# A fused cross-attention and segmented self-attention layer on one core: the cross weighted sum with its two operands exchanged, and GpSimd's rotary sums ahead of its clamps

## What is computed

```python
q, k, v = query @ Wq + bq, key_in @ Wk + bk, key_in @ Wv + bv        # split in 16 heads of 8
scores = einsum('bhqd,bhkd->bhqk', q, k) / sqrt(8)
scores = 0.5 * scores * mask + 0.5 * scores
attn = softmax(clip(scores, -50, 50), axis=-1)
context = einsum('bhqk,bhkd->bhqd', attn, v)                         # 128 queries, 77 keys
x = layernorm(query + context @ Wo + bo) * gamma + beta
```

## Time and profile before

| | us |
|---|---|
| median of 3 runs | 1788.41 |
| lowest and highest | 1788.29, 1788.67 |
| the profiled execution's own time | 1788.83 |
| its span in the trace | 1787.0 |
| TensorE matmul busy | 1626.6 (91%) |
| VectorE busy | 1205.8 (67%) |
| GpSimd busy | 837.2 (47%) |
| ScalarE busy | 779.9 (44%) |

### The profile page before, as it was taken

One profiled execution on the slowest core, in us unless ns is written; L12 is line 12 of the kernel. 1 busy time (PEld: TensorE's weight loads), 2 busy tenths in 40 slices (PEclk: granted clock), 3 DMA queues, 4 the chain that ended last, 5 costly groups with the idle time before them and its releaser, 6 DMA issues.

```text
span 1787.0 us, 61340 instructions
## 1 busy us (share of the span) xinstructions
PE 1626.6 (91%) x23267; PEld 1398.3 (78%) x23267; DVE 1205.8 (67%) x3087; ACT 779.9 (44%) x1869; POOL 837.2 (47%) x1170
## 2 busy tenths in 40 slices
PE   4899999999999999999999999999999999999997
PEld 3687787887887877878888787877877878878776
DVE  4566766766766766766766767667667667667664
ACT  2444444444444444444444344344444444444443
POOL 3345445445445445345345445454454454454452
PEclk9999999999999999999999999999999999999999
DMA  6000000000000000000000000000000000000000
GB/s 163 13 15 11 8 13 11 8 13 11 8 13 11 8 11 9 11 11 8 13 11 8 13 11 8 13 11 8 13 11 8 13 11 8 13 11 8 13 6 6
DMA packets 32411, 25.54 MB, mean 14 GB/s; under 512 B 8117, under 2 KB 31178, under 8 KB 32266
## 3 DMA queue, kind: packets, MB, share of 16 engines
q1 hardware_dynamic: 32394, 25.30, 5.4%
HBM read 20.82 MB, written 4.46 MB: 14 GB/s over the span
## 4 chain that ended last, share of the span: by engine, by line
PE 33%; issue 33%; DVE 18%; POOL 14%; POOLq 1%; DMA 1%; DVEq 0%; SPq 0%; ACT 0%; ACTq 0%
PE psum L852 9%; PE psum L816 6%; PE psum L818 6%; POOL ra L406 5%; DVE ra L631 4%; PE psum L826 4%; DVE rb L634 4%; POOL kmask L417 2%; DVE z L640 2%; POOL st L468 2%; DVE mx L701 2%; POOL z L413 2%; POOL st L421 2%; PE psum L962 2%; PE psum L835 1%
## 5 line engine op out<-in xcount | busy, mean ns | idle before, releaser
L406 POOL TENSOR_TENSOR ra<-ra,rb 128x512 f32<-128x512 f32 x256 | 322.1, 1279 | 0.1
L701 DVE TENSOR_REDUCE mx<-psum 128x4 f32<-128x324 f32 x256 | 108.7, 487 | 198.4 <-PE psum L841 198.4
L640 DVE TENSOR_TENSOR z<-psum,wT 77x512 f32<-77x512 f32 x256 | 163.6, 678 | 99.6 <-PE psum L808 99.6
L631 DVE TENSOR_TENSOR ra<-psum,rope 128x512 f32<-128x512 f32 x256 | 175.0, 683 | 81.9 <-PE psum L800 77.5
L413 POOL TENSOR_SCALAR z<-z 77x512 f32<-77x512 f32 x256 | 152.8, 611 | 149.4 <-DVE z L640 149.4
L468 POOL TENSOR_TENSOR st<-st,nhalf 128x1 f32<-128x1 f32 x64 | 37.5, 586 | 363.3 <-DVE st L726 363.3
L523 ACT ACTIVATE z<-z 77x512 f32<-77x512 f32 x256 | 152.0, 638 | 125.3 <-POOL z L413 125.3
L852 PE MATMUL psum<-qT,kall 64*81 64x64 f32 x4096 | 176.0, 236 | 23.6 <-DVE mx L701 23.6
L826 PE MATMUL psum<-cross_w,ra 128*128 128x128 f32 x1024 | 147.7, 277 | 48.4 <-POOL ra L406 47.8
L852 PEld LDWEIGHTS psum<-qT,kall 64*81 64x81 f32 x4096 | 158.4, 148 | 36.3 <-DVE mx L701 32.0
L816 PE MATMUL psum<-z,v 77*32 77x128 f32 x2048 | 179.7, 278 | 0.7 <-DVE z L640 0.7
(11 more groups left out here) (129 smaller groups left out, 3419.1 us busy)
## 6 DMA issues: line engine op xcount, KB each, us to landing
seq_in<-in SPq DMA_DIRECT2D x64, 166.5 KB
out<-out_sb SPq DMA_DIRECT2D x64, 64.0 KB, 1.6
maskT<-in SPq DMA_DIRECT2D x64, 38.5 KB
vall<-memv_dram SPq DMA_DIRECT2D x128, 4.0 KB, 1.9
ctx_all<-in SPq DMA_DIRECT2D x5, 320.0 KB, 12.1
wqkv<-in SPq DMA_DIRECT2D x1, 1536.0 KB, 9.5
ctx_all<-in SPq DMA_DIRECT2D x3, 288.0 KB, 10.8
stage<-in SPq DMA_DIRECT2D x1, 648.0 KB
```

The costliest lines, as they stand in the source:

```text
L406: nc.gpsimd.tensor_tensor(ra[:, sl], ra[:, sl], rb[:, sl], ALU.add).then_inc(rot_ready, 1)
L631: V.tensor_tensor(ra[:, sl].rearrange("n (h d) -> n h d", h=8), p, rope[:, 0, :].unsqueeze(1).broadcast_to([S, 8, DH]), ALU.mult)
L640: V.tensor_tensor(z0[:, 4 * t:4 * t + 4, :], cross_at(f"score{t}")[0:S2, :].rearrange("k (h q) -> k h q", h=4), wT[:].unsqueeze(1).broadca ...
```

## The change

- `v0` becomes 77 x 16 heads x 9 columns: eight value columns and one of ones, set to 1.0 once; `ones0` is gone, and the set-up zeroes one tile less.
- `weigh_cross` takes 64 queries of a head's exponentials as the stationary operand (77 x 64) and the head's nine columns as the moving one, into partitions 0 to 63 or 64 to 127 of bank `pv`. That is again 32 fp32 matmuls (64 records). Each group waits for its own exponentials.
- The result has queries on partitions. `context` takes a 128 x 16 reciprocal and multiplies into a new tile `c0` (128 x 128); it now stands on VectorE ahead of the maxima's reductions.
- TensorE transposes `c0` between `maxima(1)` and `scores(0)`, and ScalarE copies the transpose into `c0T` between `values(1)` and the copy of the shift. `c0T @ Wo` stays where it was. The list of bank tasks gains `c0T`.
- GpSimd adds all four rotary pairs in a row, then does the four clamps.

```diff
@@ -34,7 +34,7 @@
 NSEG = S // SEG
 NPM, NM = 16, 16
 PRE = 1 + NPM
-VROW = HD0 * GROUP + HD0
+VROW = HD0 + 1
 KEYS = SEG + PRE
 VW = DH + 1
 DFF = 341
@@ -157,10 +157,10 @@
         k0T = sb("k0T", [D, S2])
 
         kmask = sb("kmask", [D, GROUP, S2])
-        v0 = sb("v0", [S2, GROUP, GROUP * VROW])
-        ones0 = sb("ones0", [S2, GROUP * VROW])
+        v0 = sb("v0", [S2, H, VROW])
         z0 = sb("z0", [S2, H, S])
-        rden0 = sb("rden0", [128, S])
+        rden0 = sb("rden0", [S, H])
+        c0 = sb("c0", [S, D])
         c0T = sb("c0T", [D, S])
         r0 = sb("r0", [S, D])
         t0g = sb("t0g", [S, D])
@@ -281,7 +282,7 @@
 
         cross_at, cross_fill, cross_filled, cross_free = banks(ctx, nc, psum, "cross", 0, 2, [
             ("qkv", qkv0_ready, 1, 1), *[(f"score{t}", z_ready, t + 1, 4) for t in range(4)],
-            ("pv", c0T_ready, 1, 1), ("wo", r_ready, 1, 1)])
+            ("pv", c0_ready, 1, 1), ("c0T", c0T_ready, 1, 1), ("wo", r_ready, 1, 1)])
         self_at, self_fill, self_filled, self_free = banks(ctx, nc, psum, "self", 2, 4, [
             ("xnT", xnT_lo_ready, 1, 1), ("q0", rope_ready, 1, 4), ("k0", rope_ready, 2, 4), ("v0", v_ready, 1, 2),
             ("q1", rope_ready, 3, 4), ("k1", rope_ready, 4, 4),
@@ -387,13 +388,13 @@
         @block.gpsimd
         def _(pool):
             nc.gpsimd.memset(nhalf[:], -0.5).then_inc(nhalf_set, 1)
-            for t in (v0, ones0, *vall, half_gate, tanh_gate):
+            for t in (*vall, half_gate, tanh_gate):
                 nc.gpsimd.memset(t[:], 0.0).then_inc(zeros_step, 1)
-            pool.wait_ge(zeros_step, 6)
-            nc.gpsimd.memset(ones0[:].rearrange("k (r w) -> k r w", r=GROUP)[:, :, 0:HD0], 1.0).then_inc(zeros_set, 1)
+            nc.gpsimd.memset(v0[:], 1.0).then_inc(zeros_set, 1)
+            pool.wait_ge(zeros_step, 4)
             for s in range(NSEG):
                 nc.gpsimd.memset(vall[s][:, 0:H * VW].rearrange("n (h w) -> n h w", h=H)[:, :, DH:VW], 1.0).then_inc(zeros_step, 1)
-            pool.wait_ge(zeros_step, 8)
+            pool.wait_ge(zeros_step, 6)
             for s in range(NSEG):
                 mem_col = vall[s][SEG:SEG + 1, 0:H * VW].rearrange("n (h w) -> n h w", h=H)[:, :, DH:VW]
                 nc.gpsimd.memset(mem_col, float(NM)).then_inc(zeros_set, 1)
@@ -423,17 +424,11 @@
                     if first(a):
                         pool.wait_ge(setup_dve, 4)
                         nc.gpsimd.tensor_tensor(pool_st[:, 1:2], pool_st[:, 0:1], nhalf[0:B, :], ALU.pow).then_inc(setup_pool, 1)
-                    rotated("q0")
-                    rotated("k0")
-                if c is not None:
-                    clamped(0)
-                    clamped(1)
-                if a is not None:
-                    rotated("q1")
-                    rotated("k1")
-                if c is not None:
-                    clamped(2)
-                    clamped(3)
+                    for name in QK:
+                        rotated(name)
+                if c is not None:
+                    for t in range(4):
+                        clamped(t)
                 if a is not None:
                     if first(a):
                         pool.wait_ge(setup_act, 3)
@@ -534,8 +529,7 @@
                     wait(act, (kmask_ready, c))
                     nc.scalar.activation(k0T[:], p[:, S:S + S2], ACT.Identity, bias=cols[:, BK:BK + 1]).then_inc(k0_ready, 1)
                     nc.scalar.activation(q0T[:], p[:, 0:S], ACT.Identity, bias=cols[:, BQ:BQ + 1])
-                    copy(v0[:].rearrange("k g (r w) -> k g r w", r=GROUP)[:, :, :, 0:HD0],
-                         p[0:S2, 256:384].rearrange("k (g r d) -> k g r d", g=GROUP, r=GROUP)).then_inc(qkv0_ready, 1)
+                    copy(v0[:, :, 0:HD0], p[0:S2, 256:384].rearrange("k (h d) -> k h d", h=H)).then_inc(qkv0_ready, 1)
                 if f is not None:
                     wait(act, ff_filled("hnT", f))
                     copy(hnT[:], ff_at("hnT")[:, 0:S], scale=cols[:, FW:FW + 1]).then_inc(hnT_ready, 1)
@@ -567,6 +561,10 @@
                 if a is not None:
                     turned(1)
                     values(1)
+                if c is not None:
+                    wait(act, cross_filled("c0T", c))
+                    copy(c0T[:], cross_at("c0T")[:, 0:S]).then_inc(c0T_ready, 1)
+                if a is not None:
                     act.wait_ge(shift_filled, a + 1)
                     copy(shift_b[0:2 * H, :], shift_at[0:2 * H, :]).then_inc(shift_ready, 1)
                     for t in range(4):
@@ -640,13 +638,14 @@
                     V.tensor_tensor(z0[:, 4 * t:4 * t + 4, :], cross_at(f"score{t}")[0:S2, :].rearrange("k (h q) -> k h q", h=4),
                                     wT[:].unsqueeze(1).broadcast_to([S2, 4, S]), ALU.mult).then_inc(z_ready, 1)
 
-                def context_sums():
+                def context():
                     wait(dve, cross_filled("pv", c))
-                    V.reciprocal(rden0[:], cross_at("pv")[:, S:2 * S]).then_inc(cross_step, 1)
-
-                def context():
-                    wait(dve, (cross_step, cross_steps[1]("rden0", c)))
-                    V.tensor_tensor(c0T[:], cross_at("pv")[:, 0:S], rden0[:], ALU.mult).then_inc(c0T_ready, 1)
+                    p = cross_at("pv")[:, 0:H * VROW].rearrange("n (h w) -> n h w", h=H)
+                    then(V.reciprocal(rden0[:].unsqueeze(2), p[:, :, HD0:VROW]), cross_steps, "rden0", c)
+                    if not first(c):
+                        wait(dve, cross_filled("c0T", c - 1))
+                    V.tensor_tensor(c0[:].rearrange("n (h d) -> n h d", h=H), p[:, :, 0:HD0],
+                                    rden0[:].unsqueeze(2).broadcast_to([S, H, HD0]), ALU.mult).then_inc(c0_ready, 1)
 
                 def normalised(t):
                     wait(dve, self_filled(f"pv{t}", a))
@@ -695,6 +694,8 @@
                         wait(dve, self_filled(f"k{t}T", a))
                         V.tensor_copy(kall[:, 4 * t:4 * t + 4, :, 0:SEG],
                                       self_at(f"k{t}T").rearrange("p (c s j) -> p c s j", c=4, s=NSEG)).then_inc(k_ready, 1)
+                if c is not None:
+                    context()
                 if a is not None:
                     for t in range(4):
                         wait(dve, self_filled(f"max{t}", a))
@@ -704,9 +705,6 @@
                     then(V.tensor_scalar(mt[:, 0, :], mx[:], -1.0, None, ALU.mult), self_steps, "hi", a)
                     V.scalar_tensor_tensor(out=mt[:, 1, :], in0=mx[:], scalar=-1.0, in1=mt[:, 0, :],
                                            op0=ALU.mult, op1=ALU.subtract).then_inc(mt_ready, 1)
-                if c is not None:
-                    context_sums()
-                    context()
                 if f is not None:
                     wait(dve, ff_filled("lin", f))
                     dve.wait_ge(silu_ready, f + 1)
@@ -809,13 +807,11 @@
                             if r == GROUP - 1:
                                 last.then_inc(cross_fill(f"score{g}"), 1)
 
-                def weigh_cross(*groups):
+                def weigh_cross(g):
                     for r in range(GROUP):
-                        window = slice(32 * r, 32 * (r + 1))
-                        for g in groups:
-                            mm(cross_at("pv")[32 * g:32 * (g + 1), 0:S], v0[:, g, window], z0[:, 4 * g + r, :], start=r == 0)
-                        for g in groups:
-                            last = mm(cross_at("pv")[32 * g:32 * (g + 1), S:2 * S], ones0[:, window], z0[:, 4 * g + r, :], start=False)
+                        for s in range(NSEG):
+                            h, tokens = GROUP * g + r, slice(SEG * s, SEG * (s + 1))
+                            last = mm(cross_at("pv")[tokens, VROW * h:VROW * (h + 1)], z0[:, h, tokens], v0[:, h, :])
                     return last
 
                 def turn(name):
@@ -935,10 +931,10 @@
                     turn("k1")
                 if c is not None:
                     wait(pe, cross_free("pv", c))
-                    pe.wait_ge(exp0_ready, c * 4 + 2)
-                    weigh_cross(0, 1)
-                    pe.wait_ge(exp0_ready, c * 4 + 4)
-                    weigh_cross(2, 3).then_inc(cross_fill("pv"), 1)
+                    for g in range(4):
+                        pe.wait_ge(exp0_ready, c * 4 + (g + 1))
+                        last = weigh_cross(g)
+                    last.then_inc(cross_fill("pv"), 1)
                 if a is not None:
@@ -950,6 +946,11 @@
                     pe.wait_ge(memk_ready, a + 1)
                     maxima(0)
                     maxima(1)
+                if c is not None:
+                    wait(pe, cross_free("c0T", c))
+                    pe.wait_ge(c0_ready, c + 1)
+                    nc.tensor.transpose(cross_at("c0T")[:, 0:S], c0[:], ident[:]).then_inc(cross_fill("c0T"), 1)
+                if a is not None:
                     scores(0)
```

(1 more changed line is left out.)

## The result

| | before | after |
|---|---|---|
| median, us | 1788.35 | 1810.01 |
| lowest and highest | 1787.57, 1788.67 | 1801.05, 1812.15 |
| ratio to before, 95% interval | | 1.011 [1.0081, 1.0140] |
| the profiled execution, its span | 1788.83, 1787.0 | 1801.05, 1799.3 |
| mean granted TensorE clock of the profiled execution | 0.997 | 0.889 |

The kernel became about 1% slower, where 7% faster was forecast. The executions after differ by 11 us among themselves, and those before by 1 here but by 12 over all comparisons of this study (1785.98 to 1797.91); in both the longer ones have the lower mean granted clock (0.881 at 1812.15 us against 0.889 at 1801.05, and 0.989 at 1797.91 against 0.999 at 1785.98).

What follows compares the result with a forecast made beforehand. No engine but a loop of waits bounds the kernel, 27.03 us a turn. Gains of 0.80 + 0.09 + 1.15 less 0.02 make 2.02 us a turn, 127.3 over 63 turns, plus 1.2 in turn 0: 1660 us, range 1650 to 1698.

Steps and rivals of the forecast that it cites:

- GpSimd's order: Four rotary sums before the clamps: TensorE's waits before the transposes of q1 and k1 vanish, minus 0.80 and 0.09 us per turn.
- the second wait: TensorE's wait behind v1, before the transposes of k1: 0.09 us lost per turn, forecast to go.
- The margin at the exponentials: Last exponential ends at 872.43, the weighing's last group starts at 872.70: the feed holds by 0.27 us.
- The weighing: Cross weighing's 64 records, spaced 29.6 ns by the load, take 2.07 us instead of 3.22: minus 1.15 per turn.
- Rival A: In the weighing, load and stream add up: 36.7 ns a record, 0.45 us a turn more, 1688 us; chance 0.10.
- Behind it: From weighing to scores: v1 copies delay maxima(1) by 0.03 us, reciprocal and product fit, c0's transpose loses 0 to 0.05.
- The sum of the path: TensorE's path through a turn: the gains and losses shorten it by 2.02 us, to a turn of 25.0 us.
- The sum of a turn: Whole turn: 0.80 + 0.09 + 1.15 less 0.02 = 2.02 us gained, 127.3 us over 63 turns.
- rival C: Clock falls to 1.2 GHz from the thin weighing to the second scores' end: plus 3.8 us a turn, 2028 us; chance 0.04.

## Why the prediction was wrong

**GpSimd's order: right.** The transposes of q1 start 11.87 us into the turn (845.57 less 833.70) where they started at 12.70: 0.83 for my 0.80. With the second wait the weighing starts 0.93 earlier for my 0.89, and the kernel with this half alone gained 0.92 a turn. The margin at the exponentials held: the last ends at 848.42, the last group begins at 848.68 (847.28 + 48 x 0.0291), and no wait of TensorE for them shows.

**The weighing: right in time.** (2.04 - 0.204) / 63 is 29.1 ns from start to start in the mean; I had taken 29.6 from the self-attention's weighing. It is 1.97 us for my 2.07. That the stream doesn't set it is shown by the rows from 12 to 64 columns: 29.1 ns still with 32 and 29.6 with 64. That the load does rests on these rows and on the scores, which load 81 columns at 36.9 ns; no run changed the load alone. Rival A, that load and stream add up, is out.

**Behind it: nearly right.** maxima(1) starts 0.79 us after maxima(0) instead of 0.61, so the copies of v1 hold it by 0.18, for my 0.03, since the weighing was over sooner. The reciprocal of 16 columns takes 0.26 (my 0.25). The product ends at 850.05, not ahead of the first reduction but 0.08 after it has started; even so the reductions start 0.72 us after the maxima, where it was 0.71, so the pair costs nothing:

```profile
849.37 0.26 DVE L644 RECIPROCAL rden<-psum 128x16 f32<-128x16 f32 x1 [1.22 <-PE psum L814]
849.76 0.29 DVE L647 TENSOR_TENSOR c<-psum,rden 128x128 f32<-128x128 f32 x1
849.97 1.70 DVE L702 TENSOR_REDUCE mx<-psum 128x4 f32<-128x324 f32 x4
```

The cross output product starts 19.99 us into the turn, before 22.16: a gain of 2.17, and a turn without a fall is 24.9 us for my 25.0. The sum of the path was right within 0.1 us a turn at the full clock, and the kernels with 32 and 64 moving columns measure 1662 and 1663 us for my 1660; they are other kernels, and the forecast for this one stays 150 us too low.

**The clock: the step that failed.** The sum of a turn prices every record at the full clock, and the case in which that fails stands in rival C, with 0.04. Measured were a mean clock of 0.889 and falls in 53 of 62 full turns, 2.78 us each. I had named the mechanism and the place, and then argued it away: "the old weighing ran in narrow tiles too, and from the end of v1 to the scores the kernel now has 5.5 us of such work and waits without a fall, afterwards 4.3". That compares lengths of stretches and counts the old weighing as thin work. It wasn't: it streamed 128 columns in each of 64 records. The new one has the same number of records in 1.97 us and moves nine in each; with 32 or 64 moved instead and all else the same, the clock held in every full turn of the profiled executions. The sentence "the 56 columns that drop out of the stream bring nothing" is true of the time of the weighing, and hides that they were worth the clock. The row of turn 1 with its 0.50 could have warned me: in the 12 us ahead of that fall TensorE had small products with waits between them, the longest this one of 1.59 us:

```profile
52.02 1.07 PE L785 MATMUL psum<-wqkv,memT 128*64 128x512 f32 x2 [1.59 <-ACT memv L476]
```

The full turns of the old kernel had no fall, so nothing in them showed how near they were to one.

The size in C was off too: I had the fall start with the weighing and cost 5.8 us of work. It starts 2.8 to 4.0 us after the weighing's start, where the scores are due, and a turn with a fall is 2.8 us longer in the mean (27.71 against 24.93) than one without. 53 turns by 2.78 are 147 us lost, against 62 turns by 2.10 (27.03 less 24.93), 130 us, gained. 1801 less 147 is 1654, about what the kernel with 32 columns takes at its best (1655.27).

What stays open: why a fall lasts 6.8 us in most cases and 10.2 in some, why single turns are spared, and whether the size of the stationary operand or its loads count beside the columns moved, which no run varied. For this kernel the runs show falls in 52 turns with 12 columns, in 39 with 16 and in none with 32, and they tell nothing of another.

## What to carry to other kernels

A rewrite that lets each matmul stream less saves time only as long as the clock holds: read the granted clock turn by turn after such a change, and count a stretch by what it streams, not by how long TensorE is busy in it. Where the load of the stationary operand sets the distance between matmuls, extra moving columns are free (2.04 to 2.08 us from 9 to 64) and can hold the clock (1662 us against 1810). Also try dense work inside a thin stretch and not only ahead of it: the same three passes of v1, begun 3.6 us ahead of the scores instead of 4.9, brought 83 us. And take a change with two parts apart: here the half that moved only GpSimd's work gave 3.4% by itself.

## What the runs showed of the hardware

- TensorE's clock fell from 2.4 to 1.2 GHz while TensorE was never idle for long: in the stretch of 4.3 us ahead of the fall that is shown above it had matmuls under way for 4.20 us. Busy time as the page counts it did not tell whether the clock would hold: TensorE is at 96% in the slower kernel, 91% in the one before, and 94% in that with 32 columns.
- Work of the same kind helps near the thin stretch and not elsewhere in the turn: four dense products right ahead of it gave falls in 18 of 62 turns, 13 us earlier in 55, without them 53.
- A fp32 load of 64 columns and its matmul repeat every 29.1 ns in the mean with 9 to 32 moving columns and every 29.6 with 64, in two 64-column halves on the same rows of the array. The records start in pairs, 6 to 7 ns apart, a pair every 58 to 59 ns. By the v1 passes, 512 columns in 0.23 us, 55 more columns are an estimated 25 ns more of stream in each record, and the distance grew by 0.5: loads there overlap streams. What the Trainium skill says (TensorE: Matmul & The Clock Gate, Part 3, What overlaps and what doesn't), that a load overlaps running matmuls only where the row groups differ, doesn't hold in these rows.
